# Third layer of a per-pixel expert network on 64x64 tiles of TensorE, its steps interleaved with the second layer's

## What is computed

```python
x = x + conv_block(_ln_c(x))      # sign, 3x3 convolution with signed weights, batch norm, clip to -1..1
t = _to_tokens(x)                 # (32, 3136, 64)
n = _ln_t(t)                      # layer norm over the 64 channels
feat = jnp.mean(n, axis=0)        # mean over the 32 images, (3136, 64)
w = softmax(feat @ Wr + br)       # 8 gates for each pixel position
h = relu(bn1(einsum('bfd,edh->bfeh', n, W1) + b1))
h = relu(bn2(einsum('bfeh,ehk->bfek', h, W2) + b2))
y = einsum('bfeh,ehd->bfed', h, Wo) + bo
out = t + einsum('bfed,fe->bfd', y, w)
```

## Time and profile before

| what | us |
|---|---|
| median of 3 runs | 1488.68 |
| lowest, highest run | 1487.44, 1496.91 |
| the profiled execution, its own time | 1496.05 |
| span of that execution, first to last instruction | 1493.9 |
| mean granted TensorE clock, of full speed | 0.985 |

### The profile page before, as it was taken

One profiled execution on the slowest core, in us unless ns is written; L12 is line 12 of the kernel. 1 busy time (PEld: TensorE's weight loads), 2 busy tenths in 40 slices (PEclk: granted clock), 3 DMA queues, 4 the chain that ended last, 5 costly groups with the idle time before them and its releaser, 6 DMA issues. The chain is left out here.

```text
span 1493.9 us, 33196 instructions
## 1 busy us (share of the span) xinstructions
PE 1398.6 (94%) x11864; PEld 568.9 (38%) x11864; DVE 976.9 (65%) x1599; ACT 805.9 (54%) x1139; POOL 427.1 (29%) x362
## 2 busy tenths in 40 slices
PE   3999966899999999999999999999999999999998
PEld 2666632333333333333333333333333333333332
DVE  5888853666665666665676656567565667666655
ACT  3666655455555555555555555555555455555442
POOL 7000053323313323313323312332322332322330
PEclk9999977999999999999999999999999999999999
DMA  9999732233332234333233332233332134333121
GB/s 156 173 156 147 107 50 50 49 72 70 73 66 45 49 68 74 68 60 49 51 68 74 68 68 43 50 68 74 68 74 52 35 68 74 68 68 57 38 51 26
DMA packets 360592, 105.53 MB, mean 71 GB/s; under 512 B 352656, under 2 KB 352880, under 8 KB 360560
## 3 DMA queue, kind: packets, MB, share of 16 engines
q1 hardware_dynamic: 359296, 103.49, 39.8%
q0 software_dynamic: 1264, 1.61, 0.6%
HBM read 78.97 MB, written 26.09 MB: 70 GB/s over the span
## 5 line engine op out<-in xcount | busy, mean ns | idle before, releaser
L715 ACT ACTIVATE h<-ps,bias 128x896 f32<-128x896 f32 x448 | 451.6, 1008 | 449.7 <-PE ps L532 448.7
L883 DVE SCALAR_TENSOR_TENSOR v<-ps,negb,wb 128x448 f32<-128x448 f32 x896 | 570.9, 679 | 159.4 <-PE ps L558 159.3
L532 PE MATMUL ps<-xc,w 64*64 64x448 f32 x3584 | 436.9, 551 | 14.9 <-issue 8.8
L558 PE MATMUL ps<-h,w 64*64 64x448 f32 x3584 | 431.9, 545 | 0.9 <-ACT gconst L746 0.5
L571 PE MATMUL ps<-v,wo 128*64 128x448 f32 x1792 | 362.9, 545 | 0.3 <-DVE v L883 0.2
L449 POOL TENSOR_TENSOR o<-xin,gconst 128x448 f32<-128x448 f32 x112 | 124.9, 1136 | 486.1 <-ACT gconst L746 387.6
L893 DVE TENSOR_TENSOR o<-ps,o 128x448 f32<-128x448 f32 x112 | 69.8, 623 | 251.2 <-PE ps L571 251.2
L427 POOL TENSOR_TENSOR xc<-xc,spread 128x896 f32<-128x896 f32 x56 | 126.7, 2279 | 375.1 <-DMA spread<-rs_rows 375.0
L532 PEld LDWEIGHTS ps<-xc,w 64*64 64x64 f32 x3584 | 118.0, 132 | 279.2 <-issue 277.8
L558 PEld LDWEIGHTS ps<-h,w 64*64 64x64 f32 x3584 | 133.7, 132 | 223.7 <-issue 214.1
L571 PEld LDWEIGHTS ps<-v,wo 128*64 128x64 f32 x1792 | 127.3, 136 | 192.2 <-issue 190.6
(11 more groups left out here) (142 smaller groups left out, 741.2 us busy)
## 6 DMA issues: line engine op xcount, KB each, us to landing
xa<-in_x SPq DMA_DIRECT2D x64, 392.0 KB, 6.5
xin<-in_x SPq DMA_DIRECT2D x56, 448.0 KB, 6.0
spread<-rs_rows SPq DMA_DIRECT2D x112, 224.0 KB, 4.1
out<-o SPq DMA_DIRECT2D x224, 112.0 KB, 2.5
rs_rows<-rs SPq DMA_DIRECT2D x112, 3.5 KB
rows<-in_L_ffn_g POOLq DMA_DIRECT2D x2, 256.0 KB, 5.9
rows<-in_L_ffn_v POOLq DMA_DIRECT2D x2, 256.0 KB, 6.8
cwt<-in_L_conv_weight SPq DMA_DIRECT2D x2, 144.0 KB, 2.6
```

Of the source, the lines that this page charges most:

```text
L532: last = mm(ps[64 * two:64 * two + 64, bank + ab, 0:NG], w1[half, P * q + C * two:P * q + C * two + C], xc[half, s, g // 2, ab ^ (g % 2), ...
L558: last = mm(ps[64 * i:64 * i + 64, bank + low, 0:NG], w2[rows_, Q + QUADS * i, :], h[rows_, u % 2, i, ab, :], start=True, stop=True)
L715: A(h[:, u % 2, i], ps[:, bank:bank + 2, 0:NG], ACT.Relu, bias=bias[:, 0, q:q + 1]).then_inc(h_done[i], 1)
L883: last = V.scalar_tensor_tensor(out=v[:, u % 2, ab, d, :].rearrange("p (b w) -> p b w", w=W), in0=ps[:, bank + d, 0:NG].rearrange("p (b w) ...
```

## The change

Layer 3 now splits its 128 rows: matmuls of 64x64 weights, rows 0 to 63 summed in bank 6 and rows 64 to 127 in bank 7. One unit of it is two steps (d = 0, 1), issued one unit later, each after a step of layer 2. ACT copies the upper sum to SBUF (`take_upper`), DVE adds the lower one to `o` as before, and GpSimd adds the copied one (`add_upper`); the store waits for that. Layer 1 has banks 0 and 1 alone, layer 2 has 2, 3 (ab = 0) and 4, 5 (ab = 1). The variance, the logits and the transpose of the gates borrow bank 2 (`Y`; the logits 2 and 3), the centring and the spread gates banks 4 and 5 (`Z`). The 16 small matmuls of the gates become one product on DVE (`placed`, transposed gates times a mask) and one pair of 64x64 matmuls by 448 columns. Loads of `x` come in halves, and the points of `STEADY` move.

```diff
-            t=(8, 8, 8, 8), x1=(16, 16, 16, 24), centre=(24, 32),
-            var=33, log=33, root=34, square=36, inv=40, logits=56, gate=56, wb=64)
+            t=(8, 10, 12, 14), x1=(13, 16, 17, 21), centre=(20, 28),
+            var=34, root=36, square=38, inv=(40, 41), logits=58, gate=60, turn=62, wb=64)
...
 SP           def chunk(k, s, first, left):
+                    if left > 1:
+                        sp.wait_ge(x1g_done, G * k + 2)
+                        load_half(k + 2, s, 0)
                     if not first:
                         store(k - 1, G - 1)
                     if left > 1:
                         sp.wait_ge(x1g_done, G * k + G)
-                        load_chunk(k + 2, s)
+                        load_half(k + 2, s, 1)
...
 POOL
+                def add_upper(k, g):
+                    pool.wait_ge(upper_done, G * k + g + 2)
+                    pool.wait_ge(out_done, G * k + g + 2)
+                    nc.gpsimd.tensor_tensor(og, og, upper[:], ALU.add).then_inc(sum_done, 1)
                 def chunk(k, s, first, left):
-                    for g in range(G):
+                    for g in range(G - 1):
                         add_const(k, s, g)
+                    if not first:
+                        add_upper(k - 1, G - 1)
+                    add_const(k, s, G - 1)
+                    add_upper(k, 0)
...                      norm(k + 1, 1 - s, 0), norm(k + 1, 1 - s, 1), feature(k + 1, 1 - s)
+                    add_upper(k, 1)
+                    add_upper(k, 2)
...
 PE
+                def layer3(k, u, d):
+                    if d == 0:
+                        for ab in range(2):
+                            pe.wait_ge(v_done[ab], unit + 2)
+                        if Q == 0:
+                            pe.wait_ge(out_done, G * k + g + 1)
+                            pe.wait_ge(upper_done, G * k + g + 1)
+                    for low, par in ((0, 0), (1, 1), (0, 1), (1, 0)):
+                        rows_ = slice(64 * low, 64 * low + 64)
+                        last = mm(ps[64 * par:64 * par + 64, ACC_BANKS + low, 0:NG], wo[rows_, 2 * Q + d, :],
+                                  v[rows_, u % 2, par ^ (g % 2), d, :], start=(Q == 0 and d == 0), stop=(Q == QUADS - 1 and d == 1))
...              prep: centre waits v_done[1] of unit 4 (first half) and unit 6 (second half) of the running chunk
+                    if h == at.turn:
+                        pe.wait_ge(gate_done, q + 1)
+                            pe.wait_ge(v_done[0], UNITS * (q - 1) + UNITS - 1 + 2)
+                        mm(ps[0:C, Y, 0:W], gate_w[:], ident[0:C, 0:W], start=True, stop=True).then_inc(wT_full, 1)
                     if h == at.wb:
+                        pe.wait_ge(placed_done, q + 1)
+                        pe.wait_ge(wT_done, q + 1)
                         pe.wait_ge(v_done[1], UNITS * q + 1)
-                        for n in range(PAIRS):
...
+                        for hi in range(2):
+                            last = mm(ps[64 * hi:64 * hi + 64, Z, 0:NG], to_half[:, hi, :], placed[:].rearrange("p a w -> p (a w)"),
+                                      start=True, stop=True)
...              chunk, unit u:
+                            layer1(*following, 0)
                         prep_point(prep, k, s, left, POINTS * u)
+                        layer2(k, u, 0, first, left)
+                            layer3(*before, 0)
                         prep_point(prep, k, s, left, POINTS * u + 1)
+                            layer1(*following, 1)
+                        layer2(k, u, 1, first, left)
                         prep_point(prep, k, s, left, POINTS * u + 2)
+                            layer3(*before, 1)
                         prep_point(prep, k, s, left, POINTS * u + 3)
...
 ACT
+                def take_upper(k, g):
+                    act.wait_ge(l3_done, UNITS * k + QUADS * g + QUADS + RING2)
+                    A(upper[:], ps[:, ACC_BANKS + 1, 0:NG], ACT.Copy).then_inc(upper_done, 1)
...              var: Ln as before, and a second read of the bank
+                        A(vareps[:], ps[:, Y, 0:NG], ACT.Copy, bias=LN_EPS).then_inc(var_read, 1)
...
 DVE
+                    if h == at.turn:
+                        dve.wait_ge(wT_full, q + 1)
+                        V.tensor_tensor(placed[:], ps[0:C, Y:Y + 1, 0:W].broadcast_to([C, 2 * PAIRS, W]), own_place..., ALU.mult)
...              chunk, unit u: [add_out if u is odd], point 4u, layer2_out(u, 0), points 4u+1 and 4u+2, layer2_out(u, 1)
```

More of the change, by code:

```diff
@@ L150, in metaformer_kernel @@
         s_bn = sem("s_bn")
-        x_loaded = sem("x_loaded")
+        x_loaded = [sem(f"x_loaded{p}") for p in range(STEPS)]
         t_done = sem("t_done")
@@ L243, in prep_ahead, with prep_early @@
                 prep(AHEAD, 0, 0, h)
-            for h in range(HALVES):
+        def prep_early(prep, first, end):
+            for h in range(first, end):
                 prep(STEADY, 1, 1, h)
@@ L531, in layer1, with layer2 @@
                             half = slice(64 * ab, 64 * ab + 64)
-                            last = mm(ps[64 * two:64 * two + 64, bank + ab, 0:NG], w1[half, P * q + C * two:P * q + C * two + C],
+                            last = mm(ps[64 * two:64 * two + 64, L1_BANKS + ab, 0:NG], w1[half, P * q + C * two:P * q + C * two + C],
                                       xc[half, s, g // 2, ab ^ (g % 2), :], start=True, stop=True)
                     last.then_inc(z1_full[i], 1)
-                def layer2(k, u, ab, last_unit, left):
+                def layer2(k, u, ab, first, left):
                     unit, Q = UNITS * k + u, u % QUADS
@@ new lines, in layer2 @@
+                    if ab == 0 and u == 0:
+                        pe.wait_ge(placed_done, k + 1)
+                        pe.wait_ge(wT_done, k + 1)
+                    if ab == 0 and u == 1 and left:
+                        pe.wait_ge(var_read, k + 2)
+                    if ab == 0 and u == UNITS - 1 and left:
+                        pe.wait_ge(logits_read, k + 2)
+                    if ab == 1 and u == 0:
+                        pe.wait_ge(g_done, k + 1)
+                    if ab == 1 and left > 1 and u in (5, 7):
+                        pe.wait_ge(xc_done, STEPS * k + 2 * STEPS + (1 if u == 5 else 2))
@@ L599, in prep @@
                         pe.wait_ge(feat_done, q + 2)
+                        if at is STEADY:
+                            pe.wait_ge(v_done[0], UNITS * (q - 1) + UNITS - 2 + 2)
+                        else:
+                            pe.wait_ge(var_read, 1)
+                        pe.sem_inc(logits_free, 1)
                         for par in range(2):
-                            last = mm(misc[0:W, E * par:E * par + E], feat[:, par, :], wr[:], start=True, stop=True)
+                            for low in range(2):
+                                rows_ = slice(64 * low, 64 * low + 64)
+                                last = mm(ps[0:W, Y + low, E * par:E * par + E], feat[rows_, par, :], wr[rows_, :], start=True, stop=True)
@@ L798, in _ @@
                 step(V.tensor_copy(identb[:], ident[0:64, 0:64]))
+                places = ident[0:C, 0:2 * E].rearrange("p (a h n) -> p a h n", a=2, h=2)
+                step(V.tensor_reduce(to_half4[:].rearrange("p a h -> p (a h)"), ident[0:C, 0:2 * E].rearrange("p (r n) -> p r n", n=PAIRS), AX.X, ALU.add))
+                step(V.tensor_tensor(to_half4[:, 0, :], to_half4[:, 0, :], to_half4[:, 1, :], ALU.add))
+                for hi in range(2):
+                    V.tensor_copy(to_half[:, hi, :], to_half4[:, 0, hi:hi + 1].broadcast_to([C, C]))
+                V.tensor_tensor(own_place[:].rearrange("p n a -> p a n"), places[:, :, 0, :], places[:, :, 1, :], ALU.add)
                 for hi in range(2):
```

261 lines of the change are left out of this document (135 added, 126 removed).

## The result

The changed kernel takes 1507.93 us (median; 1506.16 to 1510.81), the kernel before 1489.47 beside it. The ratio is 1.0117, with a 95% interval of 1.0078 to 1.0155: it is 1.2% slower, where 1434 us was forecast, 3.7% faster. The profiled execution took 1507.65 us, its span 1505.7.

A forecast was written before the change was run, and what follows sets the result against it. TensorE's second-stage steps, 0.75 us apart, bound the kernel. A chunk falls from 44.60 to 42.6 us (39.86 of steps, 2.75 of waits); 28 chunks give 56, 1 comes back: 1488.7 - 55 = 1434 us, range 1400 to 1468.

The forecast's parts named there:

- 28 chunks: 56 us: Last line of the sum: each of 28 chunks takes 42.6 us, 2.0 less than now, 56 us in all.
- the sum of the steps after: TensorE's steps in a changed chunk: 52 at 0.75 us plus small extras, 39.86 us, 4.74 under now.
- the start: Longer first chain from logits to gates, with GpSimd's add at the end: 1 us back in all.
- the 0.3 summed for the logits: Wait 2: TensorE's logits in unit 6 wait for GpSimd's feature, between 0 and 0.9 us, taken as 0.3.
- the rival at 0.79: Layer 3's 16 steps take 0.79 us each: 0.64 more a chunk, 43.2, 1452 us; chance 0.05.
- Wait 3: VectorE reads the logits before v(6, 1), so TensorE's centring waits 0.47 us for that bank.
- Wait 4: Softmax, its exponential behind both centring reads on ACT, precedes v(7, 0); the gates' transpose waits 1.08 us.
- wait 5: After the transpose, VectorE does placed and v(7, 1); TensorE's spread gates wait 0.72 us.
- No stalls at the boundary: Rival: waits 3 to 5 at a chunk's end don't bite; chunk 40.3 to 41, 1368 to 1388 us; chance 0.13.
- The late chain over SP: Rival: SP's row of stores and loads delays norm and logits; 1453 to 1487 us, chance 0.09, or slower, 0.05.
- `x1` meets GpSimd: Rival: VectorE's last x1 waits on a GpSimd instruction, up to 1.3 us a chunk: 43.9, 1470 us; chance 0.08.

The follow-up runs named there:

- e1: Changed kernel with TensorE's chunk loop written out, no backward branch on TensorE: 1474.83 us, ratio 0.987 to the kernel before.
- e11: Changed kernel with four chunks instead of two in TensorE's loop body (3734 instructions, five jumps): 1481.12 us, ratio 0.9911.
- e3: Kernel before with 12 idle semaphore increments on TensorE after each unit's first layer-2 step (body 1877): 1691.06 us, ratio 1.1307.
- e6: Kernel before with 6 idle semaphore increments on TensorE after each unit's first layer-2 step (body 1781): 1556.59 us in one run.
- e7: Changed kernel with layer 3 of groups 1 to 3 back on 128x64 tiles (body 1678): 1525.45 us, ratio 1.0219.
- e8: Changed kernel, already covered TensorE waits cut, ScalarE preparing the next chunk first, group 3's layer 3 on 128x64 tiles (body 1772): 1503.45 us, 1.0057.
- e4: Changed kernel with TensorE's loop written out and the softmax's exponential ahead of the centring reads on ScalarE: 1453.35 us, ratio 0.9722.
- e12: Changed kernel with the last x1 one point earlier, at point 20 instead of 21: 1503.85 us, ratio 1.0083.

## Why the prediction was wrong, point by point

**What failed** is the last line of the sum, "28 chunks: 56 us": it multiplies the gain of one chunk by all of them, and takes each added instruction as costing its time on the array alone. The part "the sum of the steps after" says that layer 3 has "twice the matmuls" for the same 16 steps, and prices them by the 0.75 us of a step alone; the instructions themselves stand in the sum at nothing. With what the gates give back it is 40 matmuls more in the loop's body, 160 of the 185 added instructions by the count above, and they moved the body over a limit that the kernel before kept to. Each of 11 jumps then costs 5.1 us (e1 and e11 took them away, e3 and e6 brought them into the old kernel, e7 with a body of 1678 has one stall in eleven jumps). No rival held it either: all of them were about engines, banks and transfers, and none about the program's length. The profile's page of before had the number to ask from: 21 instruction packets for a kernel whose loops were known to be long.

The page "Runtime: NRT & Kernel Launch" of the Trainium skill ("Instruction fetch mechanics") says that a taken branch whose target is outside the current window of two pages stops the engine until the target page is fetched, and that code is fetched in blocks of 16 KiB, 256 instructions. The traces agree on the stall, with 2.8 to 3.3 us of idle time at each jump of the changed kernel, and on the blocks, with 2.00 MB in 122 packets, 16.4 KB each. They do not agree on the two pages: the kernel before jumps back over 1685 instructions, 6.6 such blocks, and reads none from 400 to 1340 us. The same section gives TensorE 2048 instructions; e8 has the stalls at 1772 by this count. In both the measurement decides.

**How the 74 us of the miss divide** (1434 to 1508), from the chunks of the two traces: the jumps 11 x 5.14 (47.74 less 42.6) = 56.5; the sixteen other chunks, 0.09 over 42.6 each, 1.4; the average chunk before was 44.53, not the 44.60 of the one that was read, which over 27 distances is 2; the start 5; the last chunk and the end, 46.7 now and 46.5 before, where some 2 less was forecast, 2; and 7.4 because the profiled execution of before lay that much above the median, while that of after lies at its own. Together 74. The 7.4 is partly the chance of three executions: beside the later runs the kernel before had medians of 1493.1 to 1493.9, 4 to 5 us above 1488.68.

**Right, by its steps:**

- A short chunk: 42.58 (790.60 to 833.18), forecast 42.6, from 44.60. That it agrees to 0.02 is in part luck: the 0.3 summed for the logits did not come, and about as much was lost in steps that follow at more than 0.75 (823.09 to 823.98, 0.89). Layer 3 at 0.75, so the rival at 0.79 falls. Plain units 4.51, forecast 4.5.
- Wait 3: 784.57 to 785.73 is 1.16, a wait of 0.41; forecast 0.47.
- Wait 4: forecast from the centring's start (828.32) were the exponential at 2.64, its last softmax instruction ended at 3.44, the transpose at 4.83. Measured 2.65, 3.44 and 4.86. Timeline of ScalarE, where the earlier trace rows has the same three:

```profile
829.36 0.92 ACT L764 ACTIVATE xc<-ps 128x896 f32<-128x896 f32 x1
830.17 0.91 ACT L766 ACTIVATE spread<-ps 128x896 f32<-128x896 f32 x1
830.97 0.21 ACT L784 ACTIVATE gate_e<-gate 56x16 f32<-56x16 f32 x1
```

- And of VectorE, with wait 5's chain in it:

```profile
831.59 0.17 DVE L993 TENSOR_TENSOR gate_w<-gate_e,gate_s 56x16 f32<-56x16 f32 x1
831.76 1.27 DVE L943 SCALAR_TENSOR_TENSOR v<-ps,negb,wb 128x448 f32<-128x448 f32 x2
...
833.50 0.62 DVE L997 TENSOR_TENSOR placed<-ps,own_place 64x448 f32<-64x448 f32 x1 [0.47 <-PE ps L641]
```

- Wait 5: 790.60 to 792.98 is 2.38, forecast 2.40. The idle time read there is 0.58 of a forecast 0.72, and 0.78 to 0.88 of a forecast 1.08 at wait 4: the distances were right, and the rest is the modelled end of the matmul ahead.

**Off in size:** the logits, forecast to wait 0.3, start at the step's distance (782.88 to 783.67, 0.79), since `feature` is early enough. And the start: the first transpose comes at 250.87 instead of 245.09, 5.8 later against about 1 forecast. There the first chunks' centrings follow each other at the half clock (granted clock 0.50 from 236 to 250 us and 0.55 from 250 to 258, where the kernel before has 0.79 and 1.00); timeline of TensorE:

```profile
242.85 1.75 PE L614 MATMUL ps<-xin,centre 64*64 64x448 f32 x8
246.50 1.77 PE L614 MATMUL ps<-xin,centre 64*64 64x448 f32 x8 [1.90 <-issue]
248.01 0.55 PE L634 MATMUL ps<-wr,feat 64*56 64x8 f32 x8
250.87 0.43 PE L641 MATMUL ps<-ident,gate_w 64*64 64x56 f32 x2 [2.31 <-DVE gate_w L993]
```

The second centring waits for ScalarE's reads of the first, and the logits stand behind both; before, they were at 243.13. The forecast counted only the chain from logits to gates.

**The other rivals:** *No stalls at the boundary* falls: waits 3 to 5 are all there, and taking one away gave 21.5 us (e4). *The late chain over SP* would show as a wait of the logits for `feature` in every chunk. From 250 to 1460 us there is one such wait, of 0.2 us, and the short chunks keep to 42.7:

```profile
PE ps L634 <- POOL feat L454: 0.2, 1, 0.2
```

The kernel did get slower, but not by this. *`x1` meets GpSimd*: it does, in 21 instructions, but the short chunks, which have as many, are at 42.7, where this rival had 43.9; e12 is 4 us better, with intervals that overlap.

**Left open:** the exact limit between 1685 and 1772, why e7 with 1678 stalls at one jump, and why code that is written out costs the old kernel about 15 us, and 0.76 a chunk in the changed one, though it never jumps.

## What to carry to other kernels

When a change adds instructions to a hardware loop, count the instructions of the loop's body on each engine before and after, f32 matmuls as four, and look at the instruction packets in the list of DMA queues of the profile's page: few packets (21 here, against 122) mean that the loop's code is not read again at each turn, and that is a resource which the change can use up. A gain of 2 us in 44 was real, and these runs had it only with fewer jumps (four chunks a body 1481 us) or none (written out 1475, with the exponential in front 1453). Where a chunk's time alternates, look for the period of the loop first, and then for "issue" as what ended the idle time.

## What the runs showed of the hardware that was not expected

- A jump back in TensorE's loop costs 2.8 to 3.3 us of idle time in the changed kernel (1870 instructions) and 3.1 to 3.6 in e8 (1772). At 1685 no jump does, at 1678 one of eleven (4.27 us, e7). With the clock, granted at 0.57 over the next 4 us in one case and at 0.51 over some 7 in another, a jump costs 5.1 us on average.
- A body of 3734 instructions costs no more at a jump (2.9 to 3.3 us idle, e11) than one of 1870, and forward reading of 1.80 MB is nearly hidden.
- Twelve semaphore increments in a row on TensorE's queue delay the next step by 0.9 us at the median where no layer 3 stands ahead, and not at all behind a layer 3 (e3); six delay it by 0.05 (e6). They were taken to be free filler.
- Going from 64x64 tiles to 128x64 and back costs 0.11 and 0.15 us more than a step (e7); in the kernel before it was 0.16 and 0.15.
